# Shared experts of three sequences moved from their own stage into the head of a fused loop, with scatters that read their places directly

## The reference

```python
t = x.reshape(-1, DIM)                       # 4096 tokens, DIM = 256
scores = softmax(t @ gate_w.T)               # 16 experts
weights, indices = top_k(scores, 2)
for e in range(16):                          # routed experts, inner width 176
    w_e = sum(where(indices == e, weights, 0))
    y = y + swiglu(t, w1[e], w3[e], w2[e]) * w_e
z = swiglu(t, sw1, sw3, sw2)                 # shared expert, inner width 352
return y + z
# swiglu(t, wa, wb, wo) = (silu(t @ wa.T) * (t @ wb.T)) @ wo.T
```

## Time and profile before

| what | value |
|---|---|
| median of 3 runs | 1998.33 us (1993.58 to 2001.99) |
| profiled execution, its own time | 1997.82 us |
| its span, first to last instruction | 1996.1 us |
| mean granted TensorE clock | 0.959 of full |
| busy share of the span | PE 94%, PEld 71%, DVE 64%, ACT 38%, POOL 21% |
| chain that ended last | PE 42%, issue 39%, DVE 9%, POOL 7% |
| DMA | 121.03 MB, mean 61 GB/s |

### The profile page before, as it was taken

The page is one execution under the profiler, slowest core; times in us unless marked ns, Lnnn a source line. Parts: engine busy times, 40 slices in busy tenths (PEclk is TensorE's granted clock), DMA queues, the critical chain, the costliest instruction groups (busy, mean ns, idle before and its releaser), DMA issues.

```text
span 1996.1 us, 34048 instructions
## 1 busy us (share of the span) xinstructions
PE 1867.9 (94%) x10114; PEld 1413.5 (71%) x10115; DVE 1270.9 (64%) x3685; ACT 763.9 (38%) x1479; POOL 426.5 (21%) x712
## 2 busy tenths in 40 slices
PE   5999999979989999568999999999999999999998
PEld 3566666557766666346888788888878887888787
DVE  3677776536422222387777877787787778877743
ACT  1566666632223333242343333334333433433321
POOL 1243444323744444200110011001001100110000
PEclk8999999979989999677999999999999999999999
DMA  9900000001322323411101110110111011101110
GB/s 359 211 4 1 0 0 1 1 1 64 116 93 93 95 92 95 184 35 59 59 6 64 62 61 5 64 58 19 51 64 59 6 64 59 54 15 48 43 48 11
DMA packets 75230, 121.03 MB, mean 61 GB/s; under 512 B 18164, under 2 KB 59252, under 8 KB 74612
## 3 DMA queue, kind: packets, MB, share of 16 engines
q1 hardware_dynamic: 68212, 100.92, 15.9%
q0 software_dynamic: 6912, 18.92, 2.7%
HBM read 81.73 MB, written 38.08 MB: 60 GB/s over the span
## 4 chain that ended last, share of the span: by engine, by line
PE 42%; issue 39%; DVE 9%; POOL 7%; ACT 2%; DMA 1%; DVEq 0%; SPq 0%; POOLq 0%; ACTq 0%
PE bank L599 5%; PE bank L184 5%; PE bank L1151 4%; PE bank L620 4%; PE bank L1216 3%; POOL sorted_in L822 2%; PE bank L1109 2%; PE bank L193 2%; PE bank L1157 2%; PE bank L1139 2%; PE bank L1244 2%; PE bank L610 1%; PE bank L528 1%; PE bank L1704 1%; DVE comb_got L2089 1%
## 5 line engine op out<-in xcount | busy, mean ns | idle before, releaser
L184 PE MATMUL bank<-moe_xT,up_w 128*128 128x256 f32 x2304 | 552.3, 383 | 0.0
L184 PEld LDWEIGHTS bank<-moe_xT,up_w 128*128 128x128 f32 x2304 | 433.9, 190 | 69.7 <-issue 11.4
L227 ACT ACTIVATE moe_silu<-bank 128x256 f32<-128x256 f32 x288 | 110.7, 384 | 609.2 <-PE bank L184 609.2
L193 PE MATMUL bank<-down_w,moe_hT 128*128 128x256 f32 x1152 | 305.4, 388 | 3.6 <-ACT moe_y L230 2.1
L193 PEld LDWEIGHTS bank<-down_w,moe_hT 128*128 128x128 f32 x1152 | 206.0, 190 | 37.9 <-issue 7.6
L1390 DVE TENSOR_REDUCE q_slots<-bank 128x4 f32<-128x1024 f32 (+1 forms) x96 | 117.7, 1226 | 77.0 <-PE bank L1151 76.4
L1298 ACT ACTIVATE probs<-bank 128x1024 f32<-128x1024 f32 x96 | 98.2, 1023 | 99.4 <-PE bank L1157 99.4
L599 PE MATMUL bank<-up_w,moe_xT 128*128 x320 | 116.7, 488 | 0.7 <-ACT moe_xT L663 0.6
L794 DVE TENSOR_TENSOR moe_h<-moe_silu,bank 128x176 f32<-128x176 f32 x80 | 27.0, 338 | 138.6 <-issue 86.2
L326 POOL TENSOR_TENSOR moe_prstd<-moe_pmv,minus_half 128x2 f32<-128x2 f32 x16 | 11.0, 690 | 484.4 <-DVE moe_pmv L304 484.4
L1151 PE MATMUL bank<-kT,qT 16*128 16x256 f32 (+1 forms) x1024 | 114.4, 351 | 0.0
(11 more groups left out here) (296 smaller groups left out, 3233.0 us busy)
## 6 DMA issues: line engine op xcount, KB each, us to landing
up_w<-comb_rows SPq DMA_DIRECT2D x32, 768.0 KB, 5.3
comb_got<-results SPq DMA_DIRECT2D x16, 768.0 KB, 7.8
moe_rows<-sorted_in SPq DMA_DIRECT2D x80, 128.5 KB
sorted_in<-zero SPq DMA_DIRECT2D x10, 1024.0 KB, 10.3
down_w<-comb_rows SPq DMA_DIRECT2D x16, 512.0 KB, 7.2
up_w<-in_up SPq DMA_DIRECT2D x2, 3168.0 KB, 15.3
up_w<-in_up SPq DMA_DIRECT2D x2, 2304.0 KB, 11.9
results<-moe_s_y SPq DMA_DIRECT2D x16, 256.0 KB
```

The source lines that it names most:

```text
L184: last = mm(k.bank[:, UP_BANK + i % 3, half * S:(half + 1) * S], m.w_up[:, c, at + half * m.inter:at + (half + 1) * m.inter], m.xT[:, par, ...
L193: last = mm(k.bank[:, SUM_BANK, j * D:(j + 1) * D], m.hT[:, i % 3, j * P:(j + 1) * P], m.w_down[:, m.expert(i), :], start=(i == 0 and j == ...
L227: nc.scalar.activation(m.silu[:, i % 3, :], k.bank[:, UP_BANK + i % 3, 0:S], ACT.Silu).then_inc(m.silu_ready, 1)
```

## The change

Of the 16 sequences' shared experts only the first 13 (`EARLY`) are computed in `SparseMoe`. The other three are computed by new steps in the head of `Tail`: "l_norm", "l_turn", "l_up" (three chunks), "l_h" (three), "l_down", listed among the head's own steps. They use `Moe`'s buffers and `Tail`'s PSUM banks, with one buffer for the hidden values and one for the result in place of two. "l_end", between periods 0 and 1, waits for their stores to land. The scatters of the 32 tiles are spread over the 27 chunks of sequences 4 to 12. Their indirect DMAs take the places straight from the table `places`: the copy and the dummy operation on GpSimd go. Row buffers: four in place of two.

```diff
+PAIR_ROWS = 4
+EARLY = 13
 def shared_steps(chunks):
     yield "norm", 0, 0
     yield "turn_x", 0, 0
+    places = chunks * (EARLY - SCATTERS_FROM)
     tile = 0
-    for t in range(B):
+    for t in range(EARLY):
         for c in range(chunks):
...
-            if t >= SCATTERS_FROM and tile < TILES:
+            place = chunks * (t - SCATTERS_FROM) + c + 1
+            while place > 0 and tile < -(-TILES * place // places):
                 yield "scatter", tile, 0
                 tile += 1
-    yield "down", B - 1, 0
+    yield "down", EARLY - 1, 0
...
-        self.place = sb("moe0_place", [P, 4], U32)
-        self.pairs = sb("moe0_pairs", [P, 2, 2, ROW])
+        self.pairs = sb("moe0_pairs", [P, PAIR_ROWS, 2, ROW])
...
         if what == "scatter":
-            par = t % 2
-            if begun(t - 1):
-                dve.wait_ge(m.scattered[par], (t - par) * 16)
+            row = t % PAIR_ROWS
+            if t >= PAIR_ROWS:
+                dve.wait_ge(m.scattered[row], 2 * 16 * (t // PAIR_ROWS))
             for j in range(2):
-                normalise(m.pairs[:, par, j, 0:D], t)
-            v.tensor_copy(m.pairs[:, par, :, D].bitcast(U32), cols(k.pair_no, t, 2)).then_inc(m.rows_ready, 1)
+                normalise(m.pairs[:, row, j, 0:D], t)
+            v.tensor_copy(m.pairs[:, row, :, D].bitcast(U32), cols(k.pair_no, t, 2)).then_inc(m.rows_ready, 1)
...
         if what == "scatter":
-            par = t % 2
+            row = t % PAIR_ROWS
             pool.wait_ge(m.rows_ready, t + 1)
-            chain.link(g.tensor_copy(m.place[:, 2 * par:2 * par + 2], cols(m.places, t, 2)))
-            g.tensor_tensor(k.pool_spare[:, 0:1], k.minus_half[:, 0:1], k.minus_half[:, 0:1], ALU.add)
             for j in range(2):
-                at = bass.IndirectOffsetOnAxis(m.place[:, 2 * par + j:2 * par + j + 1], 0)
-                g.indirect_dma_start(m.sorted_in, at, m.pairs[:, par, j, :], None).then_inc(m.scattered[par], 16)
+                at = bass.IndirectOffsetOnAxis(m.places[:, 2 * t + j:2 * t + j + 1], 0)
+                g.indirect_dma_start(m.sorted_in, at, m.pairs[:, row, j, :], None).then_inc(m.scattered[row], 16)
...
+def late_tensor(k, m, pe):
...
+        if what == "l_turn":
+            pe.wait_ge(s.xn_ready, t + 1)
+            pe.wait_ge(s.y_read, t)
+            for f in range(KD):
+                for j in range(SEQ_TILES):
+                    last = nc.tensor.transpose(k.bank[:, SUM_BANK, (f * SEQ_TILES + j) * P:(f * SEQ_TILES + j + 1) * P],
+                                               moe.xn[:, j, f * P:(f + 1) * P], k.ident[:])
+            last.then_inc(s.xT_full, 1)
+        if what == "l_up":
+            w, lo = s.wide(c), E * 2 * s.inter + c * P
+            pe.wait_ge(s.xT_ready, m.turns + n + 1)
+            if n > 0:
+                pe.wait_ge(s.h_ready, m.up(t - 1, c) + 1)
+            for half in range(2):
+                for f in range(KD):
+                    last = nc.tensor.matmul(k.bank[0:w, UP_BANK + c, half * S:(half + 1) * S],
+                                            s.w_up[:, f, lo + half * 2 * s.inter:lo + half * 2 * s.inter + w],
+                                            moe.xT[:, t % 2, f, :], start=(f == 0), stop=(f == KD - 1))
+            last.then_inc(s.up_full, 1)
+        if what == "l_down":
+            pe.wait_ge(s.h_ready, m.up(t + 1, 0))
+            for j in range(SEQ_TILES):
+                for c in range(s.shared_chunks):
+                    w = s.wide(c)
+                    last = nc.tensor.matmul(k.bank[:, SUM_BANK, j * D:(j + 1) * D], moe.hT[0:w, c, j * P:(j + 1) * P],
+                                            s.w_down[0:w, 2 * E + c, :], start=(c == 0), stop=(c == s.shared_chunks - 1))
+            last.then_inc(s.y_full, 1)
+        if what == "l_end":
+            pe.wait_ge(s.y_read, B)
...
+def late_scalar(k, m, act):
...
+        if what == "l_up":
+            w = s.wide(c)
+            act.wait_ge(s.up_full, m.up(t, c) + 1)
+            if n > 0:
+                act.wait_ge(s.h_ready, m.up(t - 1, c) + 1)
+            nc.scalar.activation(moe.silu[0:w, c, :], k.bank[0:w, UP_BANK + c, 0:S], ACT.Silu).then_inc(s.silu_ready, 1)
+        if what == "l_down":
+            act.wait_ge(s.y_full, m.turns + n + 1)
+            if n > 0:
+                act.wait_ge(s.stored[(t - 1) % 2], 16 * ((t - 1) // 2 + 1))
+            nc.scalar.copy(moe.y[:].rearrange("p j d -> p (j d)"), k.bank[:, SUM_BANK, :]).then_inc(s.y_read, 1)
...
+def late_vector(k, m, dve):
...
+        if what == "l_h":
+            w = s.wide(c)
+            dve.wait_ge(s.silu_ready, m.up(t, c) + 1)
+            if n > 0:
+                dve.wait_ge(s.y_full, m.turns + n)
+            k.nc.vector.tensor_tensor(moe.hT[0:w, c, :], moe.silu[0:w, c, :], k.bank[0:w, UP_BANK + c, S:2 * S],
+                                      ALU.mult).then_inc(s.h_ready, 1)
...
+def late_sync(k, m, sp):
...
+        if what == "l_down":
+            sp.wait_ge(s.y_read, t + 1)
+            sp.dma_start(s.shared_rows(t), moe.y[:]).then_inc(s.stored[t % 2], 16)
...
     def head(self):
-        for what, t, i in (("c_fetch", 0, 0), ("c_sum", 0, 0), ("c_sum", 0, 1), ("c_norm", 0, 0), ("c_fetch", 1, 0),
-                           ("experts", 0, 0)):
+        a, b, c = range(EARLY, B)
+        yield "c_fetch", 0, 0, 0
+        for what, t, i in (("l_norm", a, 0), ("l_turn", a, 0), ("l_up", a, 0), ("c_sum", 0, 0), ("l_up", a, 1), ("c_sum", 0, 1),
+                           ("l_up", a, 2), ("l_h", a, 0), ("c_norm", 0, 0), ("l_h", a, 1), ("c_fetch", 1, 0),
+                           ("experts", 0, 0), ("norm", 0, 0), ("l_h", a, 2), ("l_norm", b, 0), ("norm", 0, 1),
+                           ("l_down", a, 0), ("turn_x", 0, 0), ("l_turn", b, 0), ("feat", 0, 0), ("l_up", b, 0), ("feat", 0, 1),
+                           ("l_h", b, 0), ("l_up", b, 1), ("bcdt", 0, 0), ("l_h", b, 1), ("l_up", b, 2), ("turn_dt", 0, 0),
+                           ("dt", 0, 0), ("table", 0, 0), ("conv", 0, 0), ("one_plus", 0, 0), ("l_h", b, 2), ("table", 0, 1),
+                           ("dt", 0, 1), ("conv", 0, 1), ("l_norm", c, 0), ("dt", 0, 2), ("table", 0, 2), ("l_down", b, 0),
+                           ("gate", 0, 0), ("conv", 0, 2), ("l_turn", c, 0), ("gate", 0, 1), ("conv", 0, 3), ("l_up", c, 0),
+                           ("silu", 0, 0), ("l_up", c, 1), ("c_sum", 1, 0), ("l_h", c, 0), ("l_up", c, 2), ("c_sum", 1, 1),
+                           ("l_h", c, 1), ("c_norm", 1, 0), ("turn_c", 0, 0), ("turn_c", 0, 1), ("l_h", c, 2),
+                           ("norm", 1, 0), ("norm", 1, 1), ("turn_x", 1, 0), ("l_down", c, 0), ("dt", 0, 3), ("turn_dA", 0, 0),
+                           ("xdt", 0, 0)):
             yield what, t, t % 2, i
...
-        for t in (0, 1):
-            yield from self.period(t, t % 2)
+        yield from self.period(0, 0)
+        yield "l_end", B, 0, 0
+        yield from self.period(1, 1)
```

More of the change, by code:

```diff
@@ new lines, in late_scalar, with step @@
+def late_scalar(k, m, act):
+    nc, s, moe = k.nc, m.sparse, m.moe
+    def step(what, t, par, c):
+        n = t - EARLY
+        if what == "l_turn":
+            act.wait_ge(s.xT_full, m.turns + n + 1)
+            nc.scalar.copy(moe.xT[:, t % 2].rearrange("p c t -> p (c t)"), k.bank[:, SUM_BANK, :]).then_inc(s.xT_ready, 1)
+        if what == "l_up":
[9 more added lines that the diff above has]
+            nc.scalar.copy(moe.y[:].rearrange("p j d -> p (j d)"), k.bank[:, SUM_BANK, :]).then_inc(s.y_read, 1)
+        if what == "l_end":
+            for stored in s.stored:
+                act.wait_ge(stored, 16 * B // 2)
+    return step
@@ L2188, in head @@
     def head(self):
-        for what, t, i in (("c_fetch", 0, 0), ("c_sum", 0, 0), ("c_sum", 0, 1), ("c_norm", 0, 0), ("c_fetch", 1, 0),
-                           ("experts", 0, 0)):
-            yield what, t, t % 2, i
-        for what, i in (("norm", 0), ("norm", 1), ("turn_x", 0), ("feat", 0), ("feat", 1), ("bcdt", 0), ("turn_dt", 0), ("dt", 0), ("table", 0),
-                        ("conv", 0), ("one_plus", 0), ("table", 1), ("dt", 1), ("conv", 1), ("dt", 2), ("table", 2),
-                        ("gate", 0), ("conv", 2), ("gate", 1), ("conv", 3), ("silu", 0)):
-            yield what, 0, 0, i
@@ L2259, in load @@
             load_experts()
-    go_through(m, sp, one_of(combine_sync(k, m.combine, sp), load, moe_sync(k, m.moe, out, sp)))
+    go_through(m, sp, one_of(combine_sync(k, m.combine, sp), load, moe_sync(k, m.moe, out, sp), late_sync(k, m.late, sp)))
 SEQS_FIRST, REST_LOADS = 2, 4
```

96 lines of the change are left out of this document (60 added, 36 removed).

## The result

The first series gave the changed kernel a median of **2011.88 us** (2003.51 to 2016.00, 20 runs), beside 2002.03 for the kernel before in the same series: ratio 1.0043, interval 1.0030 to 1.0056. The forecast of 1990 and its range to 2003 missed that, though the difference lies within the half per cent that had the largest chance. The same source, run again in further sets, gave 1990.74, 1994.35 and 1993.15 on three chips and 2009.89 and 2007.80 (two loads) on a fourth. So there are two results, and the study is about what lies between them.

A forecast was written before the change was run, and what follows sets the result against it. TensorE, at 9 tenths from about 950 us on, was taken as the bound, so only earlier stages could pay. Gain 19.4 before the blocks, cost 11 in the head: -8.4, 1990 us against the median 1998.33; range 1981 to 2003.

The forecast's parts named there:

- the half per cent that had the largest chance: Whole kernel: a time within about 0.5%, 10 us, of the kernel before; chance 0.52, against 0.39 faster and 0.09 slower.
- Before the blocks: Stage before the routed blocks: scatters at 2.6 us a tile, VectorE supplying one in 2.4, fetch at 563.2; gain 19.4 us.
- rival 3: Scatters before the blocks don't quicken: gain there only 6.5 us, +4.5 in all, 2003 us; chance 0.09.
- rival 2: Clock stays at half through the head: first decay matmul 36 us late, +16.6 in all, 2015 us; chance 0.07.
- The lock: Scatter stage: GpSimd and VectorE exclude each other over the shared port; 13 us of the gain would go; discounted, within rival 3.
- The head: Head of the fused loop: three sequences' added work delays its chain; cost 11 us, between 6.5 and 15.
- The single milestones: Steps of the head's chain, late by 6.4, 4.4, 6.1, 8.6 and, at the first decay matmul, 10.2 us (12.6 if clock falls).
- The clock: TensorE in the head: full clock from the first sequence's up chunks, about 831.5 us; a possible fall around the gates.
- rival 4: A mixed head, with two clock falls or a late store: head costs 15 to 19 us, about 1996 us; chance 0.12.
- Table loads: ScalarE in the head: two more table switches, 1.28 us a load without the skill's drain of 1.38; otherwise 2.8 worse.
- SP's fetch for sequence 2: Head, SP's queue: the fetch waits behind the third store, going out near 880 instead of 862.63, with 10 us to spare.
- The sum: Whole kernel: -19.4 before the blocks and +11 in the head make -8.4 us, so 1990; 1986 to 1994 has chance 0.50.

The follow-up runs named there:

- e6: The changed kernel run again without an edit, on chip 13: 1990.7 us, kernel before 2000.4.
- e1: The changed kernel with the old scatter code (copy of the places, spare addition, two pairs of row buffers), on chip 10: 2006.4 us, kernel before 2001.2.
- e8: The kernel before with places read directly, still two pairs of row buffers and all 16 sequences, on chip 13: 1993.2 us, kernel before 2000.4.
- e5: The kernel before with the new scatters alone (direct places, four pairs of row buffers), all 16 sequences, on chip 10: 1991.9 us, kernel before 2001.2.
- e9: The changed kernel without an edit, on chip 12: 2009.9 us, kernel before 2002.2.
- e11: The kernel before with the new scatters alone (direct places, four pairs of row buffers), as e5 but on chip 12: 2006.2 us, kernel before 2002.2.
- e10: The changed kernel with two pairs of row buffers in place of four, on chip 12: 2009.3 us, kernel before 2002.2.
- e12: The file of e9, the unedited changed kernel, loaded once more on chip 12: 2007.8 us, kernel before 2002.2.
- e3: The changed kernel with two pairs of row buffers in place of four, on chip 10: 1997.4 us, kernel before 2001.2.

## Why the prediction was wrong, and where it was right

**Before the blocks, gain 19.4 us.** This is the step that failed for the first series: there the gain against the profile before was 151.0 - 148.5 = 2.5 us, and a tile of scatters took 3.10 us (99.1 / 32) where 2.6 stood. On the three other chips the front stage is 131.6, 131.8 and 132.0, a gain of 19.4, 19.2 and 19.0. Its parts held there: DMAs 1.27 us apart (1.30 taken), a first one of 1.89 (1.22 taken), GpSimd the bound without a break, fetch 1.7 us after GpSimd's last DMA (567.67 against 566.01). What failed is the sentence that VectorE can supply a tile in 2.4 us. It rested on 8.62 us a sequence, which holds only while TensorE's signals come when its records end. In the first series they came up to 11.8 us late, on chip 12 up to 12.7, the multiplies with them, and the rows behind the multiplies in VectorE's queue; GpSimd ran dry for 19 us. What holds the signals up stays open. No rival had this: rival 3 (2003) also has a small gain (6.5), but by another road, for the DMAs did quicken, and is 9 us short; rival 2 (2015) is nearer by number alone, for the clock did rise in the head.

**The lock.** The Trainium skill (SBUF — State Buffer, Who interferes with whom) has GpSimd and a VectorE operation that needs the shared port pair exclude each other. No sign of a lock is in the trace for these scatters: in e6 the DMAs took 956 to 1892 ns with a median of 960, with 64 normalisations on VectorE beside them, and only the first two (1.89, 1.43 us) were over 1.1. Whether these normalisations need that pair no run shows, so this isn't a test of the rule. This rival was rightly discounted. Rival 3's arithmetic is what e1 measured, though: a gain of 6.5 (151.0 - 144.5) with the copy kept, and 5.2 us slower in all, where 4.5 stood.

**The head, cost 11 us.** Right in size. In the first series the tail is 1189.6 against 1178.2, 11.4 more; on one chip, the changed kernel has 1187.1 (e6) and the one with all sequences 1175.5 (e8), 11.6 more. But the tail has two levels some 3 us apart in either kernel (1175.5 and 1178.0 to 1178.2; 1186.3 to 1187.1 and 1189.5 to 1190.1), so on one chip the difference of two profiles ranges from 8.4 to 12.1. The single milestones came earlier than I laid them out. From the timeline of e6:

```profile
800.80 15.26 SPq L2251 DMA_DIRECT2D comb_got<-results  x2
...
820.89 0.60 PE L1816 MATMUL bank<-ident,ssm_xn 128*128 128x128 f32 x4
...
831.82 0.29 PE L1841 MATMUL bank<-ident,feat_bc 72*128 72x72 f32 x2
...
854.10 0.73 DVE L2027 TENSOR_SCALAR ssm_xn<-x,ssm_mv,ssm_rstd 128x256 f32<-128x256 f32 x2 [0.80 <-POOL ssm_rstd L2173]
...
860.75 0.39 PE L1889 MATMUL bank<-dAT,sel 24*128 24x256 bf16 x2 [0.72 <-ACT dAT L1969]
```

Counted from each kernel's own first fetch: first transposes 20.1 against 14.9, 5.2 late (6.4 forecast); dt 31.0 against 28.1, 2.9 (4.4); end of the convolution 43.5 against 39.0, 4.5 (6.1); norm of sequence 1, 53.3 against 46.8, 6.5 (8.6); first decay matmul 59.95 against 50.26, **9.7** (10.2 to 12.6). It stands at 860.75; 860 was forecast, and that the two agree so well is partly luck, for e6's front stage starts 4.4 us later (436.04 against 431.61) and its blocks are 2.2 us shorter.

**The clock.** It rose among the first up chunks, as taken: the 24 records of line 917 in e6 span 7.64 us, where three times eight at full clock would be 5.2 (three of 1.73) and at half 10.5, and the down projection behind them takes 2.86, full clock. In both profiles it fell twice more, around the second down projection (twelve records took 4.55 us in e6 and 5.49 in the first series; I had placed a fall later, around the gates) and around the third (4.14 in e6, where 2.76 stood in the sum). Two falls were rival 4's condition, yet its cost of 15 to 19 us didn't come: the earlier milestones made up for them, and no row foretold that, so the hit is in part luck. Rival 2 (half clock throughout) is out.

**Table loads.** In the head of the first series the load of the exp table starts at 844.80, takes 1.28, and its function follows at 846.10:

```profile
844.80 1.28 ACT L1953 ACT_TABLE_LOAD   x1
...
846.10 0.22 ACT L1953 ACTIVATE s_e<-s_mn 128x16 f32<-128x16 f32 x1
```

The drain of 1.38 that the Trainium skill (ScalarE: Activation LUTs, What ACT_TABLE_LOAD costs) adds isn't there, and the measured head fits the sum without it.

**Nothing else moved.** Blocks 234.4 against 235.3. SP's fetch for sequence 2, now behind the third store, went out 59.3 us behind the head's first fetch (873.03 against 813.70), where I had allowed 62.

**The sum** was -8.4 us. On the chips without late stretches it was -9.7, -6.4 and -5.8 (medians against before), mean -7.3, and 1990 forecast against 1990.7 to 1994.4. The sum was sound there; what it lacked is a term for a stall that the profile before doesn't show. What it didn't ask is which part of the change earns the gain: e5 has it without the moved sequences.

## What to carry to other kernels

A stage in which three engines stand nearly level hands a stall of one to all of them: 33 to 41 us of ScalarE's waiting for late signals lengthened the changed kernel's front stage by some 16 us here. When a waiting engine has no named releaser, compare the signal's own stamp with the record of the instruction that raised it before blaming the one that waits, and with the records behind that one before calling the work late. Count the events that two traces of one program hold: where they differ, the traces weren't taken under the same conditions. And run a new version on more than one chip, with the old one beside it: a difference of under 1% can have both signs.

Price what a move frees and what it costs in the same row: 10.3 us out of a stage (142.1 - 131.8) and 8.4 to 12.1 into the head is no gain, which the quicker scatters hid.

## What the runs showed of the hardware

- On one chip of the five with a known number, and in the first series, TensorE's signals come up to 12.7 us (e9) after the ends of their matmul records while 64 indirect DMAs run beside it (24 to 41 us of nameless waits in all), at times four within 0.25 us (e11). Signals of the other engines were on time. On four other chips none was late, with the same programs. The cause isn't known. It doesn't hang on four pairs of buffers against two (e9, e10), nor on the tight order against the loose (e9, e11), nor on one load against another (e9, e12). Not settled: whether a GpSimd instruction between the DMAs prevents it.
- The same runs' traces hold 428 to 506 semaphore events between the first and the last scatter where the others hold 1263 to 1379. Not settled: whether the recording holds the signals up, or one cause does both.
- Instruction fetches, which the trace lists as DMA packets of 16 KB and 8 KB: those of 16 KB took 0.92 to 1.79 us in either kind, so slow fetches don't explain it.
- A GpSimd scatter of 128 rows costs 0.96 us of the engine and is 0.30 us from the next; a linked operation between two pairs adds 0.28 us a tile (91.1 against 82.3 us for 32), the copy with the addition 0.42 (95.7).
- The first two scatter DMAs took 1.89 and 1.43 or 1.44 us in every profile of the changed kernel; in the kernel before, e3, e5 and e11 the longest took 1.22.
- The same head added 8.4 to 12.1 us (two profiles of one chip compared), with late signals in the front stage or without. TensorE's signals were in time there, though DMAs of other kinds ran beside it.
